# Where the normalised rows are made: VectorE or ScalarE, in twelve layer norms of a two-layer block

## The reference, cut to what matters

```python
def _layernorm(x, axis=-1, eps=1e-05):
    m = jnp.mean(x, axis=axis, keepdims=True)
    v = jnp.var(x, axis=axis, keepdims=True)
    return (x - m) / jnp.sqrt(v + eps)

x = L0_attn_x                                          # (2, 1024, 512) float32
h = _layernorm(x) * (1 + ca) + sa;  x = x + ga * _L0_attn_ref(h, ...)
h = _layernorm(x) * (1 + cb) + sb;  x = x + gb * _L0_ffn_ref(h, ...)     # MLP, hidden 2048
h = _layernorm(x) * (1 + ca) + sa;  x = x + ga * _L1_attn_ref(h, ...)    # a recurrence over time
h = _layernorm(x) * (1 + cb) + sb;  x = x + gb * _L1_ffn_ref(h, ...)     # MLP, hidden 1408
```

## Time and profile before

| | us |
|---|---|
| median of 3 runs (lowest, highest) | 1370.51 (1368.22, 1380.48) |
| the profiled execution's own time | 1372.74 |
| its span, first to last instruction | 1371.0 |
| PE busy in the span | 1163.5 |
| DVE busy | 890.7 |
| ACT busy | 539.4 |
| GpSimd busy | 170.7 |

### The profile page before, as it was taken

The page is one execution under the profiler, slowest core; times in us unless marked ns, Lnnn a source line. Parts: engine busy times, 40 slices in busy tenths (PEclk is TensorE's granted clock), DMA queues, the critical chain, the costliest instruction groups (busy, mean ns, idle before and its releaser), DMA issues. The chain is left out here.

```text
span 1371.0 us, 13544 instructions
## 1 busy us (share of the span) xinstructions
PE 1163.5 (85%) x4554; PEld 617.6 (45%) x4599; DVE 890.7 (65%) x1647; ACT 539.4 (39%) x1147; POOL 170.7 (12%) x151
## 2 busy tenths in 40 slices
PE   6657898777648888899898997889898899989897
PEld 5425765665423334443344433344443344434443
DVE  3466547667754665688767886658877478765454
ACT  2342546444415423633415534135442363421321
POOL 3000100000002113111212112121210100010100
PEclk9766855555559999999999998999999999989999
DMA  8400002433153610011000101012220001100000
GB/s 262 143 31 16 1 1 78 137 123 108 31 201 119 190 40 0 16 31 54 24 0 16 31 23 47 8 32 59 91 62 8 1 24 62 39 1 31 0 31 31
DMA packets 38821, 75.57 MB, mean 55 GB/s; under 512 B 3702, under 2 KB 7286, under 8 KB 38624
## 3 DMA queue, kind: packets, MB, share of 16 engines
q1 hardware_dynamic: 37760, 72.50, 16.2%
q0 software_dynamic: 992, 2.21, 0.7%
HBM read 66.16 MB, written 8.54 MB: 54 GB/s over the span
## 5 line engine op out<-in xcount | busy, mean ns | idle before, releaser
L1400 PE MATMUL g_g<-h,wt 128*128 128x512 f16 x1728 | 407.5, 387 | 1.6 <-DVE hid L1576 1.6
L1400 PEld LDWEIGHTS g_g<-h,wt 128*128 128x128 bf16 (+1 forms) x1728 | 170.7, 99 | 228.9 <-issue 40.1
L1412 PE MATMUL g_d<-wt,parts 128*128 128x512 bf16 (+1 forms) x830 | 200.3, 381 | 11.3 <-DVE parts L1581 6.7
L1348 PE MATMUL g_o<-xmix,w_kvr 128*128 128x512 f32 x384 | 180.2, 613 | 6.5 <-ACT hf L1763 5.5
L1805 ACT ACTIVATE parts<-hid 128x512 f16<-128x512 f32 x108 | 68.0, 629 | 283.8 <-DVE hid L1576 283.8
L1569 DVE SCALAR_TENSOR_TENSOR hid<-th,g_g 128x512 f32<-128x512 f32 x108 | 73.6, 681 | 163.2 <-ACT th L1798 163.2
L1412 PEld LDWEIGHTS g_d<-wt,parts 128*128 128x128 f16 x864 | 83.4, 98 | 123.0 <-issue 16.2
L1906 POOL TENSOR_TENSOR acc<-acc,sqh 128x512 f32<-128x512 f32 x52 | 74.9, 1441 | 337.8 <-ACT sqh L1811 337.8
L1348 PEld LDWEIGHTS g_o<-xmix,w_kvr 128*128 128x128 f32 x384 | 74.8, 197 | 89.0 <-issue 73.2
L1581 DVE TENSOR_TENSOR parts<-hid,parts 128x512 f16<-128x512 f32 x108 | 81.8, 758 | 30.5 <-ACT parts L1805 30.5
L646 PEld LDWEIGHTS sc<-gatedw,LT 128*128 128x128 f32 x320 | 65.9, 281 | 35.0 <-DVE gatedw L997 21.7
(11 more groups left out here) (277 smaller groups left out, 1686.8 us busy)
## 6 DMA issues: line engine op xcount, KB each, us to landing
wmod<-in_wmod SPq DMA_DIRECT2D x12, 1024.0 KB, 7.1
w_raw<-in_wt SPq DMA_DIRECT2D x24, 512.0 KB, 4.1
w_kvr<-in_w SPq DMA_DIRECT2D x48, 256.0 KB, 2.6
xmix<-in_codes SPq DMA_DIRECT2D x16, 528.0 KB, 4.1
codes_f<-xmix SPq DMA_DIRECT2D x16, 264.0 KB, 2.2
gates<-in_x SPq DMA_DIRECT2D x4, 1024.0 KB, 5.6
x<-in_x SPq DMA_DIRECT2D x4, 1024.0 KB, 10.7
xmix<-in_wo SPq DMA_DIRECT2D x4, 1024.0 KB, 5.2
```

The source lines that it names most:

```text
L1348: mm = nc.tensor.matmul(dst[:], w1[:, n % 4, k], xmix[:, w, k], start=(k == 0), stop=(k == KD - 1))
L1400: mm = nc.tensor.matmul(pg[i][:], wide[:, k, o:o + P], h16[f % 2][:, s, k], start=(s == 0 and k == 0), stop=(s == 1 and k == KD - 1))
L1412: mm = nc.tensor.matmul(pd[j][:], parts16[:, t % 3, s, j * P:(j + 1) * P], wd[:, m, :], start=(m == 0 and s == 0), stop=(done and s == 1))
```

## The change

The rows xn are made by ScalarE, by `activation(Identity, scale, bias)` with the two columns `rstd[:, j]` and `nmr[:, j]`, in the thirds in which VectorE made them. VectorE keeps the making of `nmr`, at its old place, now into one of two buffers in turn, and no longer waits for the result itself: ScalarE does, through the counter `steps`. Ahead of `nmr`, VectorE waits until the rows of the norm two before have been made. The wait for the last transposes of the norm before moves with the rows to ScalarE. On ScalarE the rows come first in their third among the MLP norms, and ahead of `modulated1`, `earlier` and `evacuated` among the attention norms; those of x0 come right after `y_columns(0)`.

```diff
-    nmr, ysum = sb("g_nmr", [P, NJ]), sb("g_ysum", [P, NJ])
+    nmr, ysum = sb("g_nmr", [P, 2, NJ]), sb("g_ysum", [P, NJ])
...
         def norm_rows(key):
-            root, n, x = wait_root(key), norm_no[key], xs[key[1] % NG]
-            c.link(nc.vector.scalar_tensor_tensor(nmr[:], mv[:, :, 0], -1.0, root, ALU.mult, ALU.mult))
-            if n:
-                wait_full(dve, norms[n - 1][1], KD - 1)
-            for j in range(NJ):
-                nc.vector.tensor_scalar(xn[:, j], x[:, j], root[:, j:j + 1], nmr[:, j:j + 1],
-                                        ALU.mult, ALU.add).then_inc(xn_ready, 1)
+            root, n = wait_root(key), norm_no[key]
+            if n >= 2:
+                dve.wait_ge(xn_ready, (n - 1) * NJ)
+            c.did(nc.vector.scalar_tensor_tensor(nmr[:, n % 2], mv[:, :, 0], -1.0, root, ALU.mult, ALU.mult))
+            nmr_no[key] = c.n
...
+        def norm_rows(key):
+            n, x, root = norm_no[key], xs[key[1] % NG], rstd[:, root_no[key]]
+            act.wait_ge(steps, nmr_no[key])
+            if n:
+                wait_full(act, norms[n - 1][1], KD - 1)
+            for j in range(NJ):
+                nc.scalar.activation(xn[:, j], x[:, j], ACT.Identity, scale=root[:, j:j + 1], bias=nmr[:, n % 2, j:j + 1]
+                                     ).then_inc(xn_ready, 1)
...
                     s -= 7
+                if s == 2:
+                    norm_rows(("x", f))
                 if 3 <= s < 5:
...
                 a = q - ATT[i]
+                if a == 1:
+                    norm_rows(("y", i))
                 if 2 <= a < 4:
...
         y_columns(0)
+        norm_rows(("x", 0))
         for k in range(KD):
             modulated(0, k)
```

More of the change, by code:

```diff
@@ L1285, in freed @@
         return side_free[use[key] % 2]
-    root_no, var_no, add_no, code_no = {}, {}, {}, {}
+    root_no, var_no, add_no, code_no, nmr_no = {}, {}, {}, {}, {}
     norms = sorted([(PREP[f] or 0, ("x", f)) for f in range(2 * NG)] + [(ATT[i], ("y", i)) for i in range(NG)])
```

## The result

Nine runs of the changed kernel have a median of 1381.69 us (1376.34 to 1383.18), nine of the kernel before 1370.51 (1367.3 to 1380.48). The ratio of the means is 1.0064, 95% interval 1.0035 to 1.0094: slower by 8.8 us, within 4.8 to 12.9 (the medians lie 11.2 apart). The profiled execution took 1382.16 us, 9.4 more than the one of before; its span is 1380.1 us.

A forecast was written before the change was run, and what follows sets the result against it. Bound: PE idle in eleven norms on the chain statistics, power, nmr, rows, transposes. Terms 3.60 + 1.10 - 0.70 - 2.8 + 0.95 + 0 + 0.89 + 2.6 = +5.6 us on the median 1370.51 gave 1376.1 us; range 1366 to 1387.

The forecast's parts named there:

- clock rival: Behind nine longer waits for rows the low clock lasts longer: 1395 us if full, 1385 at half the norms; chance 0.12.
- The row: Each ScalarE row takes 0.80 us, four in a row 2.90 us against 1.91 on VectorE.
- From ACT to PE: PE follows an ACT result 0.05 us after its end, against 0.14 behind DVE rows: +0.90 us where nothing covers the rows.
- x3: At this norm `mixed` starts 1.64 us earlier and its matmuls gain 1.13 us from the clock: -2.8 us.
- x4: At this norm the take-out of k and the tanh wait behind the rows on ScalarE: +0.95 us.
- y3: At this norm, no square in layer 1: +0.89 us for rows, and the clock falls low for another 2.6 us.
- y0 to y2: At these norms ScalarE's rows start behind its square, but the slow DVE case goes: +0.37 us each, 1.10 in all.
- x2: At this norm the first transposes lose 0.90 us, but `modulated` and the third block's transposes run 0.71 earlier: net -0.70 us.
- x5: At this norm PE is held by other work, so the rows stay hidden, by 7 us: 0.
- fast row: Rows as fast as a one-column activation: -0.36 us at eleven norms, -4.0 us, 1372.1 us; chance 0.12.
- DVE as the true bound: Freed DVE time lets its chain run ahead, so norms inside attention work gain: some -10 us, 1361 us; chance 0.10.
- ACT's queue at x4 and x6: Tanh 3 to 5 us late, with the gate bank and next tile: +2 to +4 us, 1379; no separate chance, part of range.

The follow-up runs named there:

- split31: Kernel before, with VectorE making rows 0 to 2 of every norm and ScalarE row 3 at the same time: 1364.85 us, ratio 0.9965.
- x23_act: Kernel before, with ScalarE making the rows of x2 and x3 only, VectorE those of the other ten norms: 1364.86 us, ratio 0.9962.
- mixed: Kernel before, with x2 and x3 rows on ScalarE alone, elsewhere three rows on VectorE and the fourth on ScalarE: 1364.93 us, ratio 0.9963.
- x23_dve: Kernel before, with ScalarE making the rows of all norms but x2 and x3: 1380.49 us, ratio 1.0075.

## Why the prediction was right or wrong

The time lay in the range and the change was slower but within 1%, as forecast. The forecast was +5.6 us, measured were +8.8 (4.8 to 12.9), 9.4 between the profiled executions. The waits were forecast well and the clock was not; that the time stayed in the range owes something to the range, which took in the lower half of the clock rival.

- **The row.** 0.80 us forecast from two rows of other forms, 0.805 measured; four in a row 2.90 and 2.94. Shown, and split31 shows that this serial time is what counts.
- **From ACT to PE.** I took 0.05 us and so +0.90 at an exposed norm. The rows at x3 end at 830.36 and PE starts at 830.50 (fence below), 0.14, the same as behind DVE. The 0.05 holds for another piece of PE's work, the products that follow `hf` (833.07 to 833.13). All of x0, x1, x3, x4, y3, x6 and x7 lost 1.01 or 1.02 us.
- **y0 to y2.** +0.37 forecast, +0.48, +0.47 and +0.50 measured. The mechanism holds: ScalarE begins behind the square, and GpSimd's addition, free of its neighbour on DVE, takes 1.26 us instead of 1.53. The timeline after:

```profile
548.30 0.62 ACT L1818 ACTIVATE sqh<-hid 128x512 f32<-128x512 f32 x1
...
548.82 2.92 ACT L1757 ACTIVATE xn<-x,g_nmr,g_rstd 128x512 f32<-128x512 f32 x4
548.99 1.26 POOL L1918 TENSOR_TENSOR acc<-acc,sqh 128x512 f32<-128x512 f32 x1 [0.82 <-ACT sqh L1818]
...
551.88 1.94 PE L1309 MATMUL g_o<-ident,xn 128*128 128x128 f32 x8 [5.82 <-ACT xn L1757]
```

- **x2.** -0.70 forecast; -0.7 in x23_act. In the changed kernel the slip has grown by 1.7 us when this norm starts, from the low clock at 658 us, and the transposes of x2 themselves then ran at the low clock (1.93 us, where they took 1.06 before and 1.07 in x23_act). The prediction had no clock term at x2.
- **x3.** -1.64 forecast for the waits and -1.13 for the clock, -2.8. The timeline after answers to the earlier trace rows:

```profile
827.42 2.94 ACT L1757 ACTIVATE xn<-x,g_nmr,g_rstd 128x512 f32<-128x512 f32 x4 [2.80 <-DVE g_nmr L1472]
...
830.26 0.62 ACT L1812 ACTIVATE parts<-hid 128x512 f16<-128x512 f32 x1
...
830.50 1.94 PE L1309 MATMUL g_o<-ident,xn 128*128 128x128 f32 x8 [4.79 <-ACT xn L1757]
...
831.63 0.78 ACT L1769 ACTIVATE h<-g_o,modv 128x512 f16<-128x512 f32 x1 [0.23 <-PE g_o L1309]
...
832.30 0.77 ACT L1770 ACTIVATE hf<-g_o,modv 128x512 f32<-128x512 f32 x1
...
833.13 5.15 PE L1348 MATMUL g_o<-xmix,w_kvr 128*128 128x512 f32 x8 [0.69 <-ACT hf L1770]
```

`mixed` starts 0.69 us after the transposes where it was 3.08, so the waits changed by +1.02 - 2.39 = -1.37. Its eight matmuls took 5.15 us instead of 5.96, -0.81. In sum -2.2.

- **x4, x5.** x4 +0.95 forecast, +1.02 at the rows and 0.2 in the transposes, which ran at the low clock throughout (1.94 us, 1.71 before): no new wait of PE came from the tanh behind the rows. x5 has no wait, as forecast.
- **y3.** The clock fell, as forecast, where it had stayed high:

```profile
1101.89 1.54 PE L1309 MATMUL g_o<-ident,xn 128*128 128x128 f32 x8 [4.20 <-ACT xn L1757]
1103.23 3.14 PE L1400 MATMUL g_g<-h,wt 128*128 128x512 f16 x8
1106.20 1.04 PE L1309 MATMUL g_o<-ident,xn 128*128 128x128 f32 x8
```

From the first transposes to the third block's, 4.31 us where it was 2.63 (1100.82 - 1098.19 in the trace before): +1.68, of 2.6 forecast. x23_act, split31 and mixed have no low stretch here, x23_dve has one.

The waits thus come to +4.2 forecast and +4.8 measured. **The term that was mis-sized is the clock**: I had it at +2.6 - 1.13 = +1.5 and only at y3 and x3. It measured +0.9 there, +6.6 behind four waits that are not for rows, at 657, 689, 876 and 1226 us, and -1.7 scattered over the rest: +5.8. Three of the four waits did not change. The clock rival looked for a longer stretch behind each longer wait for rows; of that only x7 shows a little (+0.3 us), and what happened was above all more stretches, behind waits as short as 2.01 and 0.66 us. The rivals: the fast row is refuted by 805 ns; DVE as the true bound holds at x2 and x3 and nowhere else; ACT's queue at x4 and x6 cost nothing.

Why an unchanged wait of 2.01 or 3.18 us is followed by the low level in one kernel and by the high one in another stays open. It repeats in two profiles of one kernel and moves with edits far away, and the mean clock of the executions shows that it also varies within a kernel. No run here varied only the moment of such a wait.

## What to carry to other kernels

Where an engine waits for a short serial piece, the piece's length on the engine that makes it is the cost: splitting four rows over two idle engines beat either engine alone, although the busy shares called for neither. Take work off an engine where what is queued behind it is late (x2, x3), not wherever the work is, and then add up all waits: a wait removed in one place can come back in another, as 1.9 of 2.2 us did in x23_act. With PE idle for some microseconds at a time, price the clock beside the waits, over the whole kernel: here it was as large as their own part, and work of no use given to PE while it waits was worth more than any placing of the rows.

## What the runs showed of the hardware that I had not expected

- The places of the low clock repeat in two profiles of one kernel (660, 690 and 878 us), and differ between kernels that have the same waits there. The mean clock still varies among the executions of one kernel, 0.859 to 0.866 before, and the time with it.
- In all fourteen profiles the time of `groups` is idle time, plus filling, plus half of PE's busy time at 0.50, plus 835 to 839 us.
- A product of ones and the identity in float32, 128x128, is recorded as two matmuls and took 0.232 us (4.18 / 18), where a float32 transpose of the same shape takes one record and 0.13 us (1.06 / 8).
- Filling that outlasts the wait may still pay: 18 products against 12 took some 5 us past the end of the waits, and the ratios are 0.9841 and 0.9872, with intervals that just overlap.
- A second column adds to an activation out of SBUF what the first one adds: 620 and 714 ns, and 805 with both. The Trainium skill ("ScalarE: Activation LUTs", section "What ACT_TABLE_LOAD costs") gives 799 ns by its rule, an estimate; the trace agrees.
